# Typed message rows stored as three bf16 terms, groups of 512 edges, and part of the row gathers moved into the adjacency build

## The reference, cut to what matters

```python
src = node_feature[edge_src]
parts = [jax.nn.relu(node_feature)]
for t in range(3):
    msg = jax.nn.relu(src @ W_e[t].T + b_e[t])
    msg = jnp.where((edge_type == t)[:, None], msg, 0)
    parts.append(segment_sum(msg, edge_dst, num_segments=N))
agg = jnp.concatenate(parts, axis=1)          # then one of three W_n by node type
```

## Time and profile before

| what | value |
|---|---|
| median of three runs | 6698.84 us (6689.83 to 6706.6) |
| profiled execution | 6690.94 us, its span 6689.2 us |
| granted PE clock, mean over the span | 0.93 |
| PE, DVE, POOL busy, share of the span | 85%, 70%, 27% |
| DMA | 1028.57 MB, mean 154 GB/s |

### The profile page before, as it was taken

The page is one execution under the profiler, slowest core; times in us unless marked ns, Lnnn a source line. Parts: engine busy times, 40 slices in busy tenths (PEclk is TensorE's granted clock), DMA queues, the critical chain, the costliest instruction groups (busy, mean ns, idle before and its releaser), DMA issues. The chain is left out here.

```text
span 6689.2 us, 122051 instructions
## 1 busy us (share of the span) xinstructions
PE 5658.0 (85%) x41983; PEld 3702.9 (55%) x41983; DVE 4679.1 (70%) x10318; ACT 1031.0 (15%) x1894; POOL 1809.4 (27%) x1887
## 2 busy tenths in 40 slices
PE   4398999999999688888888888874899959968896
PEld 3257999999999444444444444443555524433344
DVE  7789999999999788888888888868566650032003
ACT  0044444444444000000000000013000010000000
POOL 0011000000000477777777777720000002000200
PEclk5578999999999899999999999997999979989996
DMA  9555777777777433333333333340888737635862
GB/s 316 148 170 170 192 189 193 184 196 191 190 193 185 111 82 83 82 83 83 83 83 82 82 82 83 80 35 0 324 306 304 283 119 192 192 124 193 190 203 69
DMA packets 559193, 1028.57 MB, mean 154 GB/s; under 512 B 187721, under 2 KB 447710, under 8 KB 549578
## 3 DMA queue, kind: packets, MB, share of 16 engines
q1 hardware_dynamic: 486760, 872.14, 44.0%
q0 software_dynamic: 65392, 145.28, 9.7%
q10 hardware_dynamic: 6622, 6.38, 0.3%
HBM read 688.67 MB, written 387.65 MB: 161 GB/s over the span
## 5 line engine op out<-in xcount | busy, mean ns | idle before, releaser
L1272 POOL DMA_INDIRECT big<-typed_msgs,big x1712 | 1644.7, 961 | 2220.2 <-DMA big<-edge_fields 1729.8
L1319 PE MATMUL psum<-big 128*128 128x384 f32 x3424 | 1343.8, 515 | 331.0 <-DMA big<-typed_msgs,big 328.9
L1155 PE MATMUL psum<-big 128*128 128x98 bf16 x7936 | 1549.0, 272 | 49.2 <-DVE big L1137 38.2
L1156 PE MATMUL psum<-big 128*128 128x49 bf16 x7936 | 1535.7, 229 | 0.2 <-issue 0.2
L1157 PE MATMUL psum<-big 128*128 128x49 bf16 x7936 | 1534.8, 230 | 0.0
L1743 PE MATMUL psum<-big 128*128 128x512 bf16 (+1 forms) x4704 | 1003.1, 376 | 186.8 <-DMA big<-adj 186.8
L1319 PEld LDWEIGHTS psum<-big 128*128 128x128 f32 x3424 | 583.7, 190 | 756.6 <-DMA big<-typed_msgs,big 502.0
L1155 PEld LDWEIGHTS psum<-big 128*128 128x128 bf16 x7936 | 933.3, 118 | 104.1 <-DVE big L1137 78.3
L1156 PEld LDWEIGHTS psum<-big 128*128 128x128 bf16 x7936 | 945.1, 119 | 0.0
L1157 PEld LDWEIGHTS psum<-big 128*128 128x128 bf16 x7936 | 932.1, 117 | 0.3 <-issue 0.3
L1743 PEld LDWEIGHTS psum<-big 128*128 128x128 bf16 x4704 | 463.3, 99 | 721.9 <-DMA big<-adj 191.9
(11 more groups left out here) (294 smaller groups left out, 4630.4 us busy)
## 6 DMA issues: line engine op xcount, KB each, us to landing
wadj<-big SPq DMA_DIRECT2D x248, 784.0 KB, 13.0
big<-wadj SPq DMA_DIRECT2D x124, 1568.0 KB, 7.2
big<-adj SPq DMA_DIRECT2D x210, 896.0 KB, 4.7
adj<-big SPq DMA_DIRECT2D x62, 1568.0 KB, 5.3
big<-edge_feats SPq DMA_DIRECT2D x856, 64.0 KB
edge_feats<-in_edge_attr SPq DMA_DIRECT2D x1, 51562.5 KB, 163.2
big<-typed_msgs,big POOLq DMA_INDIRECT x1712
big<-edge_fields SPq DMA_DIRECT2D x856, 8.0 KB
```

The source lines that it names most:

```text
L1155: pe.matmul(to[:, 0:2 * NB], lo, hi_b[:, q, g, :, u], start=True, stop=False)
L1156: pe.matmul(to[:, NB:2 * NB], lo, w2_b[:, q, g, :, u], start=False, stop=False)
L1272: pool.indirect_dma_start(out=got4[:, h, u, :], out_offset=None, in_=typed_rows, in_offset=bass.IndirectOffsetOnAxis(ap=fld4i[:, h, u, IDX ...
L1319: last = pe.matmul(ps[h][:, 0:T * P], got4[:, h, u, :], hot4[:, h, u, :], start=(u == 0), stop=(u == U - 1))
```

## The change

- **Messages.** After the relu, ACT and DVE split each fp32 message tile into three bf16 terms: ACT rounds it (`s_m_hi`), DVE subtracts (`rest`), ACT rounds the rest (`middle`), DVE subtracts again (`last`). A row of `typed_msgs` becomes 3 types x 3 terms x 128 bf16, so one gathered row is 768 bytes. There are three row buffers instead of two.
- **Groups.** `U` goes from 2 to 4 tiles and `Q` from 8 to 6. `NG` becomes 456. The loop body is one turn of `TURN` = 24 groups, run 19 times.
- **One-hots.** The edge's key becomes a small integer that bf16 holds, and the typed one-hot of a group is one bf16 instruction over 4 x 384 elements (its inputs have runs of two neighbouring elements). The fp32 one-hot for the features is one instruction over 4 x 128. Three small instructions per two groups make the relative numbers (`relative`). Each of the two has `HS` = 2 slots, and the adds run two groups behind.
- **Matmuls.** Per group 4 fp32 matmuls of 128 columns for the features and 12 bf16 matmuls of 384 columns for the messages. Typed and feature sums lie side by side in `acc`, so one `add` of 512 columns replaces two.
- **Staging.** In each turn the 11 groups at odd positions below 22 are gathered during the adjacency build and stored to DRAM (`staged`). The build handles 7 of them per pair of blocks in two parts, of 4 and of 3: SP loads fields (`fields_part`), POOL gathers 4 tiles for each, SP stores the part (`store_part`). In the typed sums SP loads such a group back with one DMA of 393 KB, and POOL gathers the other 13.
- **Spread stores.** Each `wadj` store takes every fourth partition (`wadj_st[h::4]`) instead of 32 neighbouring ones; the weighted layer's copy out of PSUM undoes that order (`spread`).

```diff
-U, Q = 2, 8
+U, Q = 4, 6
...
+def is_staged(pos):
+    return pos % 2 == 1 and pos < 2 * STAGED
...
                         for h in range(4):
                             sp.dma_start(wadj[...].rearrange("(q p) x -> p q x", q=4),
-                                         wadj_st[h * 32:(h + 1) * 32, k, :, :, :].rearrange("p q s g -> p q (s g)")
+                                         wadj_st[h::4, k, :, :, :].rearrange("p q s g -> p q (s g)")
                                          ).then_inc(s_wadj_st[k], 16)
...
+                        if k == 0:
+                            store_part(sp, i, 0)
+                            if not final:
+                                fields_part(sp, i + 1, 0)
...
+            @block.gpsimd          # in the adjacency build
+            def _(pool):
+                def body(i):
+                    for h, (c0, c1) in enumerate(PARTS):
+                        at_least(pool, s_sgot, i * (16 * SPER * U) + 16 * c0 * U)
+                        pool.wait_ge(s_sfld[h], i * (16 * (c1 - c0)) + (fld_from[h] + 16 * (c1 - c0)))
+                        at_least(pool, s_sst[h], i * 16 + sst_from[h])
+                        for c in range(c0, c1):
+                            for u in range(U):
+                                pool.indirect_dma_start(
+                                    out=sgot4[:, c, u, :], out_offset=None, in_=typed_rows,
+                                    in_offset=bass.IndirectOffsetOnAxis(ap=sfld4i[:, c, u, IDX0:IDX0 + 1], axis=0)
+                                ).then_inc(s_sgot, 16)
...
+                def rest(b):
+                    dve.wait_ge(s_m_hi, b + 1)
+                    dve.tensor_tensor(mrest3[b % 2], mfull3[b % 2], mterms[b % MR][:, :, 0, :], ALU.subtract)
+                def last(b):
+                    dve.wait_ge(s_m_mid, b + 1)
+                    dve.tensor_tensor(mterms[b % MR][:, :, 2, :], mrest3[b % 2], mterms[b % MR][:, :, 1, :], ALU.subtract)
...
+                def one_hot(i, pos):
+                    h, k = pos % Q, pos % HS
+                    at_least(dve, s_mm, i * TURN + (pos + 1 - HS))
+                    dve.tensor_tensor(hot4[:, k, :, :].rearrange("p u (c r) -> p u c r", r=2),
+                                      ramp_pairs..., relk4..., ALU.is_equal)
+                    dve.tensor_tensor(hotd4[:, k, :, :], iota..., rel3..., ALU.is_equal).then_inc(s_hot, 1)
...
+                        got_wait(pe, i, pos)
                         for u in range(U):
-                            last = pe.matmul(ps[h][:, 0:T * P], got4[:, h, u, :], hot4[:, h, u, :],
-                                             start=(u == 0), stop=(u == U - 1))
+                            for r in range(TERMS):
+                                last = pe.matmul(ps[h][:, 0:T * P], got_terms[:, h, u, r, :], hot4[:, k, u, :],
+                                                 start=(u == 0 and r == 0), stop=(u == U - 1 and r == TERMS - 1))
```

More of the change, by code:

```diff
@@ L85 @@
 HROW = AROW // S2
+MR = 3
 def at_least(eng, sem, value):
@@ L109, in in_batches, with in_turns @@
         body(NB // BB, NB % BB)
[L112 to L122, removed]
+def in_turns(eng, body):
+    body(0)
+    with eng.Fori(1, NG // TURN, 1) as i:
+        body(i)
 def build(nc, x, src, dst, attr, etype, weight, ntype, w_e, b_e, w_n, b_n, w1, b1, w3, w3e, b3, out):
@@ L1055, in _, with registers @@
                     outs(*shares[n])
+        typed_rows = typed_msgs.rearrange("n (t f) -> (n t) f", t=T)
+        def registers(engine, table, first, n, most):
+            _, values = nc.values_load_multi_w_load_instructions(table[0:1, bass.ds(first, n)], engines=(engine,),
+                                                                 min_val=0, max_val=most,
+                                                                 skip_runtime_bounds_check_because="clamped where the table is made")
+            return values
         tab, at = cut(0, 2 * 5 * SLOTS // 2)
@@ L1207, in slot_free, with loaded_by @@
+        def loaded_by(i, pos):
+            return i * (16 * TURN // Q) + 16 * (pos // Q + 1)
         def slot_free(eng, done, g):
             at_least(eng, done, g + (1 - Q))
[L1211 to L1238, removed]
@@ L1275, in step @@
                             ).then_inc(s_got[h], 16)
-                in_groups(pool, step)
+                in_turns(pool, turn)
             @block.vector
@@ new lines, in turn @@
+                def turn(i):
+                    g0 = i * TURN
+                    opening = isinstance(i, int)
+                    for pos in range(TURN):
+                        if pos % Q == 0:
+                            skip = LAG if opening and pos == 0 else 0
+                            bucket = [None] * skip + list(registers(mybir.EngineType.DVE, bucket_of, g0 + (pos + skip - LAG),
+                                                                    Q - skip, NB - 1))
+                        if pos % 2 == 0:
+                            relative(i, pos)
+                        one_hot(i, pos)
+                        if bucket[pos % Q] is not None:
+                            add(g0 + (pos - LAG), (pos - LAG) % Q, bucket[pos % Q])
@@ L1307, in _ @@
+                in_turns(dve, turn)
+                bucket = registers(mybir.EngineType.DVE, bucket_of, NG - LAG, LAG, NB - 1)
+                for r in range(LAG):
+                    add(NG - LAG + r, (NG - LAG + r) % Q, bucket[r])
             @block.tensor
             def _(pe):
-                def step(g0):
-                    for h in range(Q):
-                        pe.wait_ge(s_hot, g0 + (h + 1))
-                        pe.wait_ge(s_feat[h], arrived(g0))
-                        slot_free(pe, s_acc, g0 + h)
+                pe.wait_ge(s_zero, 3)
```

246 lines of the change are left out of this document (173 added, 73 removed).

## The result

The changed kernel takes 6100.54 us (median of 4 runs, 6099.44 to 6101.45) against 6697.33 us of the kernel before beside it (4 runs): ratio 0.9108, 95% interval 0.9092 to 0.9124. A later control with 5 runs gave 0.9109 (0.9096 to 0.9122). Forecast were 6065 us and 5910 to 6240.

A forecast was written before the change was run, and what follows sets the result against it. PE was taken to become the bound of the typed sums, at 3.2 us per group. Typed sums, build and slot tables gave 6691 - 701 + 40 + 37 = 6067 us, forecast as 6065 us, range 5910 to 6240 us.

The forecast's parts named there:

- PE's group: Typed sums: 8 fp32 records and 12 bf16 matmuls with phase costs take PE 3.24 us per group, taken as 3.2.
- So PE becomes the bound, at 3.2 us: Typed sums: PE sets the pace, 456 x 3.2 = 1459 us; the block takes 1504 us against 2205, -701.
- a sign of being wrong: Typed sums: the forecast is wrong if PE waits for gathers in each turn.
- POOL's price: Gathers cost 1.26 us each, up to 1.41; in the typed sums 65.5 to 73.3 us per turn, below PE's 76.8.
- DVE charged nothing: Build: gathers beside DVE's one-hots cost DVE no time; the gather takes 1.11 instead of 0.94 us.
- rival D: Build: gathers and DVE's two-input instructions exclude each other, + 816 us of DVE work, total 6768 us; chance 0.02.
- The one-hot's rate: Typed sums: DVE's bf16 one-hot of 1536 runs at the fast rate, 0.87 us, near 0.95 us long in the profile.
- rival B: Typed sums: DVE becomes the bound, its typed one-hot at one element per cycle, + 0.8 us per group, 6202 us; chance 0.13.
- The padding: Padding gathers read one row 128 times: 49 to 86 us at the build's end, some 15 us in the typed sums.
- SP's new waits fall into its idle time: Build: SP's waits for parts of gathers, ahead of the next `adj` store, fit its queue's 1110 us of idling.
- Rival C: Build held up by DMA or SP's order: 58 us per pair instead of 52.4, + 174 us, total 6200; chance 0.15.
- The slot tables: Two DVE subtractions of 0.46 us per bucket, 45 us against 31 us idle: +37 us, bounds +15 and +60.

The follow-up runs named there:

- the control: The changed kernel run again, unchanged, beside later variants: 6104.06 us, ratio 0.9109 against the kernel before.
- the fewer gathers: The changed kernel with the four gathers at position 22 of each turn left out, a probe that skips work: 6020.44 us, ratio 0.8987.
- spread filler rows: The changed kernel with filler rows naming 512 different message rows instead of row 0: 6038.53 us, ratio 0.9014; the same edit on the kernel before: ratio 0.9989.
- the first and third groups: Two sets of four follow-up runs each, on a chip where the kernel before took 7258 and 7263 us.

## Why the prediction came out as it did

**Sign, size and place right.** 6100 against 6065, 597 us less against 632. The typed sums gave 684 us (701 forecast), the build and its drain took 57 (40), the slot tables 22 (37), the rest 11 (below 5).

**PE's group: right, a little high.** 3.07 us against 3.2. The 12 bf16 matmuls and the 8 fp32 records take 2.05 and 1.02 us to the next phase, where the sum had 2.15 and 1.09.

**"So PE becomes the bound, at 3.2 us": the wrong step.** PE has 73.7 us of work per turn, and 77.9 were taken. The bound is POOL, as the fewer gathers showed. PE waits for gathers in most turns, which comes close to what the prediction named as a sign of being wrong. What failed is POOL's price: 1.26 us per gather, at most 1.41. Both figures are those of gathers that happened to be held for little. In the earlier trace rows the gather starts 0.91 us into a one-hot of 1.21 us and so has only 0.30 us of it to wait for; all 44 that start inside such a one-hot in that trace (L317) end 0.81 to 0.82 us after it. In the earlier trace rows the fp32 one-hots beside the gathers are only 0.42 us long, so the longest gather took 1.19 us:

```profile
3529.99 1.19 POOL L1272 DMA_INDIRECT big<-typed_msgs,big  x1 [0.30 <-issue]
```

```profile
3529.93 0.43 DVE L1295 TENSOR_TENSOR big<-iota,big 128x256 f32<-128x256 f32 x1 [1.31 <-PE psum L1319]
```

So the rule stood in the trace of before; the price depends on how much of the one-hot is left when the gather starts. In the changed kernel the one-hot is 0.96 us long and each second gather starts 0.25 us into it, again and again: it takes 1.52 us, on average 1.54 us of pitch in lockstep, 80 us per turn. Two errors met: PE was put too high and POOL too low, so 24 x 3.2 = 76.8 us was close to the 77.9 measured for another reason. The time of the forecast is right there by luck; its mechanism is not.

**DVE charged nothing: right.** The build's one-hot of 2048 elements took 1.22 us, the same as without gathers (L1133 before and L1243 after, 496 times each, mean 1219 ns in both). "It is POOL that gives way" holds, and rival D (mutual exclusion at DVE's cost) falls. How far POOL gives way was undersized: the build's 868 gathers took 1.28 us on average, up to 2.02. There it cost nothing: the 28 gathers of a pair took some 46 us of its 52.2 from the first to the last, and 28 of 30 steps between pairs stayed within 0.2 us of 52.2.

The Trainium skill (SBUF — State Buffer, SBUF: two separate sides) says that an instruction of VectorE with two SBUF inputs and a GpSimd instruction that reads SBUF exclude each other for the length of whichever starts first. The traces agree in one direction, for bf16 and fp32 alike: the gather waits for the end of the one-hot in flight, 2.07 us in the longest case shown. The adds of the kernel before (L1301), which read PSUM, held none: of 142 gathers that started well inside one, 141 took under 0.96 us. The traces do not show the other direction: of the build's 496 large one-hots 411 started during a gather, and the longest took 1.24 us against 1.22 at the median. The measurement decides.

**The one-hot's rate: right.** 0.959 us, near the 0.95 named; rival B would have been 1.76 us.

The page VectorE: DVE Perf Modes of the Trainium skill (Mode 2x_1P) asks for 16-bit inputs with a step of one; with runs of two the trace has 0.96 us, with repeated single elements 1.76 us, so it agrees.

**The padding: right in kind, its drain wrong.** The build lost 29 us to it, the drain 19, the typed sums 12, by the control against the spread filler rows. The prediction had 49 to 86 in the build, less 10 for a faster drain. The drain got no shorter: 26 us before, 28 with spread filler rows, 49 in the changed kernel. The faster stores do shorten it, to 19 us with the staging undone, where the prediction had about 15. What was left out is the last part of gathered rows, which has to land and be stored as well: its store goes out 18 us after the last adjacency copy with spread filler rows (2244.83 against 2226.4) and 39 us after it in the changed kernel (2294.44 against 2255.6), where 5.5 us more go by while the last adjacency stores stand on SP behind the part before. "SP's new waits fall into its idle time" is true in mid-build (DVE and PE show no loss) and fails at the end. Rival C named the DMA engines and SP's order, but for every pair; only the last one was held up.

**The slot tables: 22 instead of 37.** DVE's two subtractions took 0.553 us each, 54 us in sum; the engine is now busy for 232 of 246 us against 203 of 234, so more of them went into idle time than I had allowed.

**The rest.** Of 11 us some 6 appear in the third and fourth layer's products over `adj`, 3 by the end of the `wadj` layer. The edit of the stores touches only the latter. The same part varied by 9 us between two profiles of the changed kernel (2274 and 2283), so these 11 us are hardly more than what varies, and no run explains them.

## What to carry to other kernels

- Count the instructions of the engine that issues gathers before those that get cheaper: with 1824 gathers instead of 1712 the cheaper matmuls were worth nothing (1.045), and moving 868 of them into a block where that engine idled was worth 904 us.
- When two engines come out close in a forecast, price each beside the new instructions, not beside the old ones; here the rival for the bound was 3 us per turn away, and the price that decided was that of a gather that starts early in a long one-hot. Look at where in the other engine's instruction each sample starts, not at its duration alone.
- Let padding name different rows: 128 reads of one DRAM row per gather cost 65 us in a kernel whose padding is 4% of the groups.

## What the runs showed of the hardware that I had not expected

**Reads of one row.** In padding groups a gather takes 1.53 us of all 16 DMA engines instead of 0.40, and the traffic beside it falls from 307 to 229 GB/s, as above.

**A chip on which the blocks with message gathers are slower.** On the chip of the first and third groups the kernel before takes 8% longer. Its build, without gathers, is the usual one, and so are the slot tables with their 45 gathers of 4 KB rows in 234 us (DVE busy for 207 us there against 203 in the earlier trace rows); in the typed sums all engines stall. The kernel before with spread filler rows, build and typed sums:

```profile
576.00:2200.00 1624.00, 1578.21 (x23802) 1523.47 (x23799) 1544.80 (x2474) 761.39 (x992) 0.00 (x0) 1.00 0.71 188
2300.00:4800.00 2500.00, 1863.57 (x6272) 964.82 (x6272) 1606.94 (x5491) 0.00 (x0) 1520.31 (x1572) 0.86 0.27 66
```

The build is that of the earlier trace rows to within 5 us of busy time on each engine, the typed sums take 2733 us instead of 2205. With the changed kernel's gathers in it, the build takes 2280 us there (spread filler rows, first group) against 1623:

```profile
600.00:2870.00 2270.00, 1685.46 (x23655) 1530.71 (x23653) 1528.97 (x2465) 754.10 (x985) 965.08 (x866) 0.74 0.57 210
```

PE's granted clock is 0.74 there, beside gaps in its work; the instructions keep their lengths (DVE's L1247 1.22 us, the message gathers 0.95 us at the median), the gaps between them grow, DVE's up to 14.9 us with no releaser on this core. Why, stays open. The same kernel with neighbouring stores took 6965 and 6647 us in two groups on this chip, so it varies as well. The changed kernel itself was not timed there; its variants that compute everything bring 3.5 to 8.5% (ratios 0.959 to 0.965 in the first group, 0.915 to 0.923 in the third), and the gathers cost time in the build. A kernel timed on one chip alone would have hidden that.
